# 192 bytes of padding in SBUF ahead of the activation buffers of a two-layer kernel's last stage

## What is computed

```python
x = u
x = x + layernorm(attn(layernorm(x)))
x = x + layernorm(ffn(layernorm(x)))

def attn(u):                       # D=256, S=16 poles, K=3, FF=672
    z = rmsnorm(u, pre_norm_w) @ in_proj_w.T
    x2, x1, v = split(short_conv(z))           # depthwise, 3 taps
    h = sum(residues * exp(log_poles * t))     # long filter
    xv = x1 * v
    y = (causal_conv(xv, h) + xv * D_skip) * x2
    y = y @ out_proj_w.T + u
    zm = rmsnorm(y, post_norm_w)
    return y + gelu(zm @ l1_w.T) * (zm @ l2_w.T) @ l3_w.T

def ffn(x):                        # H=1024; m1, m2: products of 16 tokens of x
    h = gelu(x @ W1.T + scale * (x @ m1.T) + b1)
    return h @ W2.T + scale * (h @ m2.T) + b2
```

## Time and profile before

| | |
|---|---|
| median of 3 runs | 1076.82 us (1076.62 to 1077.31) |
| the profiled execution, first to last instruction (its span) | 1076.4 us |
| TensorE matmul busy | 1052.2 us, 98% of the span |
| VectorE / ScalarE / GpSimd busy | 882 / 710 / 300 us |
| mean DMA rate | 96 GB/s |
| the last stage | from 247.1 us to the end |

### The profile page before, as it was taken

One profiled execution on the slowest core, in us unless ns is written; L12 is line 12 of the kernel. 1 busy time (PEld: TensorE's weight loads), 2 busy tenths in 40 slices (PEclk: granted clock), 3 DMA queues, 4 the chain that ended last, 5 costly groups with the idle time before them and its releaser, 6 DMA issues.

```text
span 1076.4 us, 24951 instructions
## 1 busy us (share of the span) xinstructions
PE 1052.2 (98%) x9012; PEld 1009.4 (94%) x9012; DVE 881.6 (82%) x2322; ACT 710.0 (66%) x1589; POOL 300.1 (28%) x575
## 2 busy tenths in 40 slices
PE   8899999999999999999999999989999999999998
PEld 7777888899989999999999999989999999999997
DVE  7999998874788878888887888898878888887776
ACT  6879887864456666666666665656666666666644
POOL 7677775460101111111111111111112111111111
PEclk9999999999999999999999999999999999999999
DMA  4337988987432333333333333543333333333000
GB/s 129 119 116 235 292 219 194 375 309 144 88 66 42 54 57 50 51 52 54 57 67 57 53 51 60 132 86 41 60 50 50 51 53 54 59 63 60 21 21 31
DMA packets 112491, 102.83 MB, mean 96 GB/s; under 512 B 7552, under 2 KB 103744, under 8 KB 112112
## 3 DMA queue, kind: packets, MB, share of 16 engines
q1 hardware_dynamic: 111136, 98.67, 41.9%
q0 software_dynamic: 736, 2.51, 0.7%
q10 hardware_dynamic: 496, 0.05, 0.0%
HBM read 75.75 MB, written 30.70 MB: 99 GB/s over the span
## 4 chain that ended last, share of the span: by engine, by line
PE 67%; DVE 6%; issue 2%; ACT 1%; POOL 0%; DMA 0%; SPq 0%; POOLq 0%; DVEq 0%; ACTq 0%
PE ps_ring L1546 35%; PE ps_w L1546 16%; PE ps_m L1546 9%; PE ps_o L1546 4%; PE ps_rt L1561 2%; DVE base L1368 1%; PE ps_w L1556 1%; DVE bn L1272 1%; PE ps_m L1612 1%; DVE prod L1315 0%; DVE ht_l L1284 0%; DMA base<-in_w 0%; DVE pt_l L1284 0%; POOL sc L1124 0%; DVE yrow L1507 0%
## 5 line engine op out<-in xcount | busy, mean ns | idle before, releaser
L1124 POOL TENSOR_TENSOR sc<-sc,neg_half 128x2 f32<-128x2 f32 x127 | 94.8, 746 | 677.8 <-DVE sc L1496 405.7
L1189 ACT ACTIVATE gate<-ps_ring 128x256 f32<-128x256 f32 x192 | 73.0, 381 | 127.4 <-PE ps_ring L1546 126.4
L1210 ACT ACTIVATE hid<-ps_ring,b1s 128x256 f32<-128x256 f32 x256 | 112.4, 484 | 27.7 <-PE ps_w L1546 13.5
L1546 PE MATMUL ps_ring<-mt_l,wl_h 128*128 128x256 f32 x640 | 125.8, 278 | 2.6 <-DVE mt_l L1284 2.6
L1546 PE MATMUL ps_ring<-mt_h,wl_h 128*128 128x256 f32 x640 | 125.7, 278 | 1.9 <-DVE prod L1315 1.3
L1546 PE MATMUL ps_ring<-mt_h,wl_l 128*128 128x256 f32 x640 | 125.2, 277 | 0.0
L1284 DVE TENSOR_TENSOR ht_l<-hid,ht_h 128x256 fp32r<-128x256 f32 x256 | 103.2, 423 | 16.8 <-ACT ht_h L1214 10.9
L1546 PE MATMUL ps_ring<-xt_h,we_h 128*128 128x256 f32 x512 | 103.5, 283 | 2.8 <-DVE prod L1315 2.4
L1315 DVE TENSOR_TENSOR prod<-ps_ring,gate 128x256 f32<-128x256 f32 x192 | 80.7, 421 | 24.6 <-ACT gate L1189 20.8
L1546 PE MATMUL ps_ring<-xt_h,we_l 128*128 128x256 f32 x512 | 100.2, 277 | 0.0
L1546 PE MATMUL ps_ring<-xt_l,we_h 128*128 128x256 f32 x512 | 100.2, 277 | 0.0
(11 more groups left out here) (203 smaller groups left out, 2732.8 us busy)
## 6 DMA issues: line engine op xcount, KB each, us to landing
toep_scratch<-taps_scratch SPq DMA_DIRECT2D x26, 512.0 KB, 7.5
toep<-toep_scratch SPq DMA_DIRECT2D x26, 512.0 KB, 8.5
xa<-in_x SPq DMA_DIRECT2D x16, 512.0 KB, 5.0
x_scratch<-x2c SPq DMA_DIRECT2D x16, 512.0 KB, 3.7
x2s<-x_scratch SPq DMA_DIRECT2D x32, 256.0 KB, 6.9
xa_c<-in_x SPq DMA_DIRECT2D x32, 256.0 KB, 2.7
xb_c<-in_x SPq DMA_DIRECT2D x32, 256.0 KB, 2.7
yin<-seq SPq DMA_DIRECT2D x124, 64.0 KB, 6.1
```

Source lines behind the costliest of these rows:

```text
L1124: nc.gpsimd.tensor_tensor(sc[:, to], sc[:, to], neg_half[:, 0, 0:CC], ALU.pow).then_inc(S[done], 1)
L1189: nc.scalar.activation(gate[rows_of, m % 2], ring[m % RING][rows_of, 0], ACT.Gelu_apprx_tanh).then_inc(S["gate_done"], 1)
L1210: nc.scalar.activation(hid[:, m % HIDS], block_of, ACT.Gelu, bias=b1s[:, m:m + 1]).then_inc(S["hid_done"], 1)
L1546: mm = nc.tensor.matmul(out, lhs(a, kk), rhs(b, kk), start=(j == 0), stop=(closed and j == len(todo) - 1))
```

## The change

A tensor of 48 float32 per partition, `offset`, is declared behind `scale_s`. Nothing reads or writes it. Every buffer declared after it in `phase_c` starts 192 bytes further on (table above). No instruction is added, taken away, or moved on any engine; the operand addresses are all that differs.

```diff
@@ phase_c
     RING = 4
+    OFFSET = 48
     FIRST_OUT = (14, 5, 3)
@@
         scale_s = sb(ctx, "scale_s", [P, 1])
+        sb(ctx, "offset", [P, OFFSET])
         xa = sb(ctx, "xa_c", [P, CC, D])
         xb = sb(ctx, "xb_c", [P, CC, D])
```

## The result

The changed kernel takes 1106.29 us (median of 4 runs, 1105.5 to 1106.51) against 1076.72 us (4 runs), a ratio of 1.0272 with a 95% interval of 1.0259 to 1.0285: **2.7% slower**, where no change was forecast and 1085 was the top of the range.

The account below looks back on a forecast made before the run. TensorE was taken to bound the kernel, by matmul count times distance between starts. Four address terms, 0 + 0 + 0 + 0 on a median of 1076.82 us, gave 1076.8 us, range 1069.5 to 1085.

Parts of the forecast that it names:

- What bounds the kernel: Last stage: TensorE busy for all of a 24.47 us step, so time is matmul count times distance between starts.
- the two: Paces of 256-column matmuls in the trace: short, about 113.3 ns, and long, about 118 ns, some 4.5 ns apart.
- Step 3: Distance between a product's two operands, from 64 to 256 bytes in 512: likeliest 0, bounds -7 to +17.5 us.
- `wrest` row: Trace row of six matmuls, weight blocks at 224 and 480 against rows at 288: 115 ns each, read as no change.
- all at the long pace: Step 3's upper bound: 162 matmuls x 4.5 ns in each of 21 steps, plus some 2 us: +17.5 us.
- fillers' row: Trace row of fillers loading and streaming `wout_h` from one address, 0 apart: median 283 ns, about 120 ns pace.
- half a ring apart: Operands 256 bytes apart in 512, taken as the most there can be, where the two reads would meet less.
- Steps 1 and 2: Streamed rows (114 matmuls a step) and stationary rows (92 a step) moving from 288 to 480 in 512: 0 each.
- Step 4: DMAs and other engines' operands at moved addresses: any delay stays hidden behind TensorE, 0.
- Rival A: Clash theory: operands half a ring apart meet less in SBUF, `ps_o` and `ps_m` go short; -7 us, 1070; chance 0.29.
- Rival B: Runs keep the pace they begin with and fall long: +6 us (1083) to +17.5 (1094); chances 0.15 and 0.08.
- 1 in 3: Share of long `ps_w` runs from which Rival B would decide the outcome, put at 2.2 us.

Follow-up runs that it names:

- rows_448: Padding of 448 bytes in place of the change's 192, so rows lie 0 from the weights modulo 512; 1105.66 us beside 1076.31 for the kernel before.
- rows_256: Padding of 256 bytes in place of the change's 192, so rows lie 320 behind the weights; 1077.15 us beside 1076.31 for the kernel before.
- both_192: Kernel before plus 192 bytes of padding ahead of the weight tensors, so weights and rows both move and stay 64 apart; 1077.98 us beside 1076.31.
- the mixtures: Four variants of the kernel before, with rows placed 64 or 192 behind their weights modulo 256 product by product; ratios 1.0011 to 1.0035.
- load_192: Kernel before with only the loaded rows (yt, pt, pstack, ht) at 0 from the weights modulo 256, mt and xt at 64; 1099.15 us beside 1076.73.
- mix_s: Kernel before with yt, mt and xt at 192 behind their weights, pt, pstack and ht at 64, all modulo 256; ratio 1.0016.
- rows_32: Padding of 32 bytes in place of the change's 192, so rows lie 96 behind the weights; a step takes 25.37 us, against 24.47 before.
- rows_96: Padding of 96 bytes in place of the change's 192, so rows lie 160 behind the weights; a step takes 25.35 us, against 24.47 before.

## Why the prediction was wrong, point by point

*What bounds the kernel.* Right. TensorE is busy for all of a step before and after, and the whole 28.5 us of the last stage is the number of matmuls times a longer distance between their starts. The forecast's list of what to look for named the case of a pace other than the two (109 ns or over 120), with wrong bounds as what it would mean. It is 120.0 ns, at the edge of what was named.

*Step 3, the distance of the two operands,* **is the step that failed**, twice. First, its likeliest value was taken from the `wrest` row. That row moves a 64-column load by 256 bytes, which modulo 256 is no move at all: both its blocks are at one distance from the rows, and it had nothing to say on the change. (In the changed kernel they are both at 0 and still go at 115 ns, so these short loads are no guide to the full ones there; at the other five dear places the six `wrest` matmuls do cost, 117.0 to 119.5 ns each.) Second, the bound above was "all at the long pace", +17.5 us, though the fillers' row, quoted in the same step, showed a third pace of 120 ns at distance 0. With that row as the bound it would have read: 162 matmuls from 113.3 to 120 and 44 from 117.8 to 120, 1.18 us a step, +32 us; measured 1.07 and +29.6. The price stood in the trace; it was left out since "half a ring apart" was taken for the opposite of 0, by a ring of 512 bytes that no row showed. rows_448 and rows_256 show that the ring is 256.

*Steps 1 and 2, the rows' own place,* gave 0, and alone they cost nothing: both_192 has the rows where the change has them, at 1077.98 us. But the argument behind them, that three places in 512 go at one pair of paces, was drawn from products which all have 64 or 192 between their operands, or 128 with 512 columns streamed. It could not tell place from distance, so that 0 came out right for these two steps was not earned. In step 2 the row was the same `wrest` row, which moves a loaded weight tensor and no rows.

*Step 4, DMAs and other engines.* Right. In the changed kernel they land as they did:

```profile
xb_c<-in_x SPq DMA_DIRECT2D x24, 256.0 KB, 2.7
out<-frow SPq DMA_DIRECT2D x23, 256.0 KB, 3.2
```

The rule of the Trainium skill that was set against the change there, on its page "DMA: Bandwidth & Descriptors", section "How a descriptor splits into AXI transactions", asked for 18% more beats on these transfers as an estimate; the landing times do not show it.

*Rival A* looked at the right quantity, where the two reads of a product lie to one another, with its sign turned: the dear place is the change's distance. That the two reads clash in SBUF is a way to read this; the runs show only the dependence on the addresses. Its objection, that one distance has both paces, was right and is what the mixtures ran into. *Rival B* had the sign with the wrong mechanism and too small a price. (Its "1 in 3" is a slip too: a third of its 5.8 us is 1.9, under the 2.2 that it names.) It stated that runs hand their pace on; load_192 makes the up-projection long behind a product at 120 ns, which fits, but mix_s makes it long behind a short `ps_w`, which does not.

The Trainium skill's page "TensorE: Matmul & The Clock Gate", section "Step-by-step: what each phase is for", says that TensorE has two independent read ports on SBUF, so that loading the next weights takes no read bandwidth from the running matmul. These runs do not fit with that at every pair of addresses: with the same loads and streams, 113 to 118 ns becomes 120.0 ns when the two starts are equal modulo 256. What it is that the two reads share, no run shows.

## What to carry to other kernels

In a TensorE-bound kernel with one weight load per matmul, as here with 128x128 F32R loads and 256 streamed columns (no other type or length was measured), look up the start addresses of the loaded and of the streamed operand of each product, and keep their difference at 64 or 192 modulo 256; here the other six places cost 1.5 to 2.7%. Any buffer declared ahead of them moves it, so a change that adds a few bytes of scratch can bring or take away more than it was made for: in a comparison, check that these distances stayed. And when a price is bounded by the nearest rows, ask of each what its own operands' difference is, and take the dearest row that fits the pattern as the bound.

## What the runs showed of the hardware that was not expected

- The time between the starts of 256-column F32R matmuls at the 2.4 GHz level keeps to one level over dozens of matmuls: 113.3 or 118 ns at the good distances, 120.0 ns at 0 modulo 256, all for 106.7 ns of columns. At the other five places single distances scatter (115 to 125 ns in rows_32's up-projection) around the means of the table.
- At distance 0 full loads lengthen from a median of 188 to 192 ns, and matmuls with 64-column loads stay at 115 ns. Neither holds elsewhere: at the other five dear places a full load of the up-projection has a median of 188 ns as before, at up to 120 ns a matmul (rows_32), and 64-column loads go at 117 to 119.5. So longer loads are not the price as such.
- At 0 both kinds of product come to 120.0 ns. Away from 0 and 128 it matters which operand is loaded: in rows_32 the up-projection goes at 119.9 ns and `ps_o` at 117.9, in rows_96 at 117.7 and 119.7.
- rows_256 reproduces the kernel before step by step, 24.47 us, although every activation buffer has another address.
